# NF4 rounding of feed-forward weights moved from a stage of its own into the attention's steps

## The reference

```python
x1 = layernorm(x  + self_attention(x))      # 16 heads of 32, 8 key heads, rotary, softmax
x2 = layernorm(x1 + cross_attention(x1, ctx))   # keys and values from a 128-wide latent, causal
out = layernorm(x2 + w3 @ (silu(w1 @ x2) * (w2 @ x2)))
```

```python
s = max(abs(block))                       # 11264 blocks in each matrix
q = clip(round((s - mean(s)) * qf), -128, 127)   # qf from the largest of 64 neighbouring s
step = NF4[argmin(abs(block / s - NF4))]   # one of 16 levels
w = step * (q / qf + mean(s))
```

## Time and profile before

| | |
|---|---|
| median of 3 runs | 1345.85 us |
| the profiled execution, its own time | 1342.16 us |
| its span in the trace | 1340.3 us |
| TensorE busy | 1161.6 us (87%) |
| VectorE busy | 802.0 us (60%) |
| ScalarE busy | 414.3 us (31%) |
| GpSimd busy | 233.9 us (17%) |
| first product of the attention stage | 198.59 us |
| first row maximum on VectorE | 228.22 us |

### The profile page before, as it was taken

The page is one execution under the profiler, slowest core; times in us unless marked ns, Lnnn a source line. Parts: engine busy times, 40 slices in busy tenths (PEclk is TensorE's granted clock), DMA queues, the critical chain, the costliest instruction groups (busy, mean ns, idle before and its releaser), DMA issues. The chain is left out here.

```text
span 1340.3 us, 17710 instructions
## 1 busy us (share of the span) xinstructions
PE 1161.6 (87%) x6598; PEld 734.9 (55%) x6613; DVE 802.0 (60%) x1232; ACT 414.3 (31%) x537; POOL 233.9 (17%) x134
## 2 busy tenths in 40 slices
PE   0588777799999999998999999999989399999995
PEld 0144335355454565454565565665655287878784
DVE  7899956456576557567457456466464534545444
ACT  0211111333434423544435434434423131111110
POOL 1522412145226226120001210010001000000000
PEclk9799988699999999999999999999999699999998
DMA  5210012312412313413423524423431510202010
GB/s 187 75 37 24 35 69 65 90 42 54 116 33 71 87 34 108 132 45 88 127 63 107 155 68 115 125 59 97 113 82 49 215 41 0 94 0 94 0 64 31
DMA packets 60778, 103.61 MB, mean 77 GB/s; under 512 B 19622, under 2 KB 20134, under 8 KB 59942
## 3 DMA queue, kind: packets, MB, share of 16 engines
q1 hardware_dynamic: 55286, 85.64, 22.0%
q0 software_dynamic: 4400, 16.78, 3.8%
q10 hardware_dynamic: 1024, 0.26, 0.1%
HBM read 41.29 MB, written 17.04 MB: 44 GB/s over the span
## 5 line engine op out<-in xcount | busy, mean ns | idle before, releaser
L1076 DVE TENSOR_REDUCE att_mx<-att_scores 128x2 f32<-128x1024 f32 (+3 forms) x256 | 262.3, 1025 | 260.3 <-PE att_scores L718 131.4
L959 ACT ACTIVATE att_probs<-att_scores_T 128x1024 f32<-128x1024 f32 (+2 forms) x256 | 214.4, 883 | 252.5 <-PE att_scores_T L741 131.5
L718 PE MATMUL att_scores<-att_k_stack,att_q_stack 96*128 96x512 f32 (+2 forms) x512 | 181.0, 424 | 36.2 <-DVE att_mx L1076 30.8
L759 PE MATMUL att_pv<-att_probs,att_v 128*32 128x512 f32 (+3 forms) x1024 | 207.5, 527 | 0.0
L759 PE MATMUL att_pv<-att_probs,att_ones 128*32 128x512 f32 (+3 forms) x1024 | 207.4, 527 | 0.0
L737 PE MATMUL att_scores_T<-att_q_stack,att_k_stack 97*128 97x512 f32 (+2 forms) x512 | 159.0, 414 | 5.6 <-ACT att_raw L935 5.1
L263 PE MATMUL nf_acc<-nf_steps,nf_ident 128*128 128x512 bf16 x480 | 120.0, 402 | 38.1 <-DVE nf_steps L322 37.3
L718 PEld LDWEIGHTS att_scores<-att_k_stack,att_q_stack 96*128 96x128 f32 x512 | 95.3, 200 | 81.1 <-DVE att_mx L1076 52.5
L641 POOL TENSOR_TENSOR att_o_lo<-att_pv_raw,att_o_hi 128x512 fp32r<-128x512 f32 x32 | 44.5, 1391 | 484.0 <-DVE att_o_hi L1094 484.0
L322 DVE TENSOR_SCALAR nf_steps<-nf_x 128x1536 bf16<-128x1536 bf16 x165 | 122.0, 792 | 10.9 <-PE nf_acc L263 5.1
L737 PEld LDWEIGHTS att_scores_T<-att_q_stack,att_k_stack 97*128 97x128 f32 x512 | 99.4, 198 | 48.6 <-issue 31.1
(11 more groups left out here) (172 smaller groups left out, 1868.1 us busy)
## 6 DMA issues: line engine op xcount, KB each, us to landing
att_q_stack<-att_q_hi SPq DMA_DIRECT2D x256, 64.0 KB, 2.0
att_k_stack<-att_k_hi SPq DMA_DIRECT2D x192, 64.0 KB, 2.0
att_q_stack<-att_q_lo SPq DMA_DIRECT2D x128, 64.0 KB, 2.0
att_k_stack<-att_k_lo SPq DMA_DIRECT2D x96, 64.0 KB, 2.0
nf_nat<-w_nat SPq DMA_DIRECT2D x3, 1408.0 KB, 9.0
w_nf<-nf_w_turned SPq DMA_DIRECT2D x11, 384.0 KB, 2.3
att_y<-x POOLq DMA_DIRECT2D x4, 1024.0 KB, 5.6
x_after_self<-att_y SPq DMA_DIRECT2D x4, 1024.0 KB, 5.8
```

The source lines that it names most:

```text
L718: last = T.matmul(sco[:, r, 0:width], qst[0:96, s, r, P * t:P * t + P], kst[0:96, s, r if crossed(b) else 0, 0:width], start=True, stop=no ...
L759: last = T.matmul(pv[HD * j:HD * j + HD, sums, q0:S], lhs, pt[:, r, at:at + S - q0], start=(t == 0), stop=(t == TT - 1))
L959: A.activation(pt[:, r, 1024 * h:1024 * h + w], bank[:, 0:w], ACT.Exp, scale=SCALE).then_inc(st_free, 1)
L1076: V.tensor_reduce(mx[:, p % 2, :].rearrange("p (r t) -> p r t", r=2)[:, :, t], sco[:, :, 0:P * (t + 1) if crossed(b) else S], AX.X, ALU.ma ...
```

## The change

`nf4_stage` is gone; `build` calls `attention_stage` alone, which now loads and splits the first x and the self attention's weights itself (`x0`, `w0`, two parts of 768 columns each) and takes the largest values of the weight blocks (`largest`, four reduces) between and behind its first three rotations. The scalers are quantised by VectorE inside step (0, 3) and put in order in (0, 7), with two trips through DRAM.

The weights come in a second time from the host, turned (`w_t`). GpSimd multiplies them by reciprocals in 24 pieces of 704 columns at steps 3 to 26 (`divide`), VectorE bounds each piece from below (`bound`), and SyncE stores it to DRAM before it loads the next: one buffer, `xp`. The rounding then runs in 48 rounds, at steps 8 to 27 and 33 to 60. A round loads 32 rows of 1408 columns four times over the partitions (`x4`), so that each group of 32 partitions holds the same weights. One pass compares with four limits, another one in each group; four passes cover 15. `scalar_passes` gives one of four passes to ScalarE (Sign), and three of four at p = 3, 4, 5 of the self blocks; the rest are VectorE's. TensorE adds the steps up in 16 products of 352 columns (`rounding`), VectorE scales (`scale_rounded`), SyncE stores.

```diff
+def round_of(b, p):
+    at = b * NP + p
+    u = at - NP if at < NP + SELF_ROUNDS else at - CROSS_HOME + SELF_ROUNDS if at >= CROSS_HOME else -1
+    return u if 0 <= u < ROUNDS else None
+def scalar_passes(u):
+    b, p = divmod(u + NP, NP)
+    return (0, 1, 3) if u < SELF_ROUNDS and b < B - 1 and p in (3, 4, 5) else (0,)
...
# SyncE
+            def load_piece(i):
+                if i > 0:
+                    sp.wait_ge(piece_out, 16 * i)
+                sp.dma_start(xp, w_t[:, at]).then_inc(piece_in, 16)
+                sp.dma_start(recb, rec_dram[:, None, at].broadcast_to([2, 64, PIECE])).then_inc(piece_in, 16)
+            def load_round(u):
+                if u > 0:
+                    sp.wait_ge(st_full, AT["round", u - 1] + 1)
+                sp.wait_ge(piece_out, 16 * (2 * (u // 4) + 2))
+                sp.dma_start(x4, x_nf[32 * r:32 * r + 32, at][None].broadcast_to([4, 32, CHUNK])).then_inc(rows4_in, 16)
+                if u > 0 and u != SELF_ROUNDS:
+                    store_round(u - 1)
...
# GpSimd, in each step
+                    if p < 2 and b + 1 < B:
+                        lo_of_x(b + 1, p)
+                        nxt = (b + 1, 1) if p == 0 else (b + 2, 0)
+                        pool.wait_ge(x_lo, x_half(b + 1, p))
+                        load_x(*nxt)
...
                     if p in (2, 4, 6):
                         lo_of_o(KT * b + p // 2 - 1)
+                    if piece_of(b, p) is not None:
+                        divide(piece_of(b, p))
# TensorE, behind weigh 0 and 1
+            def rounding(u):
+                pe.wait_ge(over_act, ACT_PASSES[u + 1])
+                pe.wait_ge(over_vec, VEC_PASSES[u + 1])
+                for k in range(4):
+                    for j in range(4):
+                        last = T.matmul(bank[32 * j:32 * j + 32, 0:CW], nsteps[:, 32 * k:32 * k + 32],
+                                        passes[k][:, CW * j:CW * j + CW], start=k == 0, stop=k == 3)
# ScalarE
+                A.activation((over + [x4])[k], x4, ACT.Sign, bias=limits[:, 4 + k:5 + k]).then_inc(over_act, 1)
# VectorE, in each step: passes 1 and 2 behind maxima 1, then
                     if fore:
                         maxima(*fore, 2)
...
+                    if piece_of(b, p) is not None:
+                        bound(piece_of(b, p))
+                    exceeds(u, (3,))
...
+                    early = bool(made(b + 1, p)) or p == 1
+                    if fore and early:
+                        maxima(*fore, 3)
+                    if u is not None:
+                        scale_rounded(u)
+                    if fore and not early:
+                        maxima(*fore, 3)
```

More of the change, by code:

```diff
@@ L828, in project_out, with turn_scalers, make @@
                 last.then_inc(st_full, 1)
-            def make(b, whats, part):
+            def rounding(u):
+                bank = bank_for(("round", u))
+                x4, dqb = home(u)
+                passes = over + [x4]
+                pe.wait_ge(over_act, ACT_PASSES[u + 1])
[4 more added lines that the diff above has]
+                                        passes[k][:, CW * j:CW * j + CW], start=k == 0, stop=k == 3)
+                last.then_inc(st_full, 1)
+            def turn_scalers(unit, t):
+                bank = bank_for(unit)
+                for w in range(NW):
+                    last = T.transpose(bank[0:SB, P * w:P * w + P], t[:, SB * w:SB * w + SB], ident[:, :])
+                last.then_inc(st_full, 1)
+            def make(b, whats, half):
                 if not whats:
                     return
-                what, i = (whats[part], (0, 1)) if len(whats) == 2 else (whats[0], (part,))
+                what, i = (whats[half], (0, 1)) if len(whats) == 2 else (whats[0], (half,))
                 for j in i:
@@ L842, in make @@
                         project(b, what, j)
-            pe.wait_ge(const_ok, 1)
             for what in ("q0", "k0", "q1", "v0"):
-                for part in range(2):
-                    make(0, [what], part)
-            pe.wait_ge(const_ok, CONSTS)
+                for half in range(2):
+                    make(0, [what], half)
+            pe.wait_ge(const_ok, CONSTS - 1)
             for t in range(TT):
@@ L870, in _ @@
                     if crossed(b) and p == 0:
-                        for part in range(2):
-                            make(b, values_of(b), part)
+                        for half in range(2):
+                            make(b, values_of(b), half)
                         maxima(*fore, 2)
@@ new lines, in exceeds, with scale_rounded @@
+            def exceeds(u, ks):
+                for k in ks:
+                    if u is not None and k not in scalar_passes(u):
+                        exceed(u, k)
+            def scale_rounded(u):
+                bank = wait_full(dve, ("round", u))
+                x4, dqb = home(u)
+                base = NF4[0] + sum(STEP[4 * k + h] / 2 for k in scalar_passes(u) for h in range(4))
+                dve.wait_ge(dqb_in, 16 * (u + 1))
+                if u > 0:
+                    dve.wait_ge(w_out, 16 * u)
+                V.scalar_tensor_tensor(wout, bank[:, 0:CW], base, dqb, ALU.add, ALU.mult).then_inc(round_ok, 1)
```

724 lines of the change are left out of this document (402 added, 322 removed).

## The result

| | before | after |
|---|---|---|
| median | 1345.59 us (4 runs) | 1817.2 us (4 runs, 1813.47 to 1821.6) |
| profiled execution, its own time | 1342.16 us | 1813.47 us |
| span in the trace | 1340.3 us | 1811.7 us |

The ratio is 1.35, 95% interval [1.346, 1.354]: slower by 472 us where 53 us of gain were forecast. The time lies far outside the range of 1245 to 1345.

A forecast was written before the change was run, and what follows sets the result against it. It took VectorE to bound the NF4 stage and TensorE to be 90% and 94% busy in self and cross attention. 1342.2 - 166 (start) + 75 (self blocks) + 42 (cross blocks) = 1293 us; range 1245 to 1345.

The forecast's parts named there:

- I take 352 KB to be there 3 us later: Each round's x4 load: there 3 us later, while VectorE wants it 4.4 us after the round.
- rival on a late x4: In the 48 rounds: landing 2.6 us longer loses 1.2 us each, +58, 1351 us, slower; chance 0.08.
- its pass as 1.35 us of work: ScalarE, rounding steps: one pass takes 1.35 us more in a step, and the engine is not full.
- self blocks: Blocks 0 to 3: waits for pieces and rounds add 75 us, bounds 26 and 105.
- cross blocks: 28 rounds there: 28 us plus 14 us for eight steps at p = 2 and 4, +42, bounds 20 and 75.
- The new start: Kernel start without the NF4 stage: first reduce of maxima at 62 us instead of 228, gain 166 us.
- The round: TensorE, each round: 16 products on four column groups take 0.8 us, lower end 0.6, upper end 2.35.
- The rival without overlap: TensorE's column groups don't overlap in bf16: 2.35 us a round instead of 0.8, 74 us more, 1367; chance 0.05.
- GpSimd's product last in its step: Self blocks: `bound`, pass 3, quarter 3's reduce and the round wait behind it; +6.0 us at p = 0.
- By step: Self blocks 1 and 2: added waits step by step, from 1.3 to 6.0 us, together 25 us a block.

The follow-up runs named there:

- e1_rows_first: Changed kernel with x4's copy having 32 rows outermost instead of 4 groups, limit and step tables permuted to match: 1610.4 us, ratio to before 1.198.
- e5_rec_two: e1_rows_first with a piece's reciprocals in two copies of outer dimension 64 instead of one of outer dimension 2: 1474.0 us.
- e3_pass0_last: Changed kernel, x4's copy as it was, with ScalarE's pass 0 moved from in front of exponential 2 to behind exponential 3: 1613.6 us.
- e7_wide_late_pass: e5_rec_two with the scalers once for two rounds in four copies and ScalarE's pass 0 behind exponential 3: 1384.7 us.
- e8_divide_first: e7_wide_late_pass with GpSimd's piece multiplied first (p = 3 to 5: end of the step before) and `bound` before passes 1 and 2: 1323.0 us.
- e9_big_behind: e8_divide_first with the store of y and the load of the cross attention's weights issued behind x4's copy: 1319.8 us.
- e14_best_timed: The kernel of e10_pieces_before unchanged, timed against the kernel before in five rounds: 1299.9 us, ratio 0.969.
- e10_pieces_before: e9_big_behind with SyncE storing a piece and loading the next before it loads the step's stacks: 1294.3 us.
- e11_four_engines: e10_pieces_before with x4's copy alone as in the changed kernel, 4 groups outermost: 1403.0 us.

## Why the prediction was wrong

**The step that failed.** "I take 352 KB to be there 3 us later". It stood in the rival on a late x4, which had 0.08; in the sum the wait for x4 was nothing. The rival named the right place and the price from which it decides, 1.1 us a round. But the 3 us are what the size alone gives by two copies with 128 rows outermost; the prediction shows no other working for them. Measured from issue to first use: 9.6 us in the median of the cross rounds that waited, 15.7 in the self rounds. With the order of two dimensions turned the kernel is 207 us shorter, 4.3 us for each of the 48 rounds (e1_rows_first). The page DMA: Bandwidth & Descriptors of the Trainium skill (Why a DMA increments its semaphore by 16 and not by 1, How many engines) has the rule: the number of engines is the largest up to 16 that divides the slowest dimension, longer than one, of source and destination. For [4, 32, 1408] into 128 partitions that is 4, for the reciprocals' [2, 64, 704] it is 2. Both agree with the traces: a share of 0.14 to 0.28 in the self step above where the wide copy shows 0.80, and the landing of the wide x4 in self blocks at 12.0 us behind the reciprocals as one copy and at 4.1 behind them as two (e5_rec_two). Which engines carried a copy no trace here shows. The diff shows both shapes, so this could have been read before the run.

**What I didn't think of at all.** First, that one slow copy delays the next: the reciprocals were no term of the sum, and x4 behind them took 15.7 us in the median. They cost 136 us (e1_rows_first to e5_rec_two). Second, ScalarE. The prediction counted its pass as 1.35 us of work on an engine that isn't full. It is also a wait in front of exponential 2, on which TensorE's ring of banks hangs; that alone was worth 204 us against the changed kernel (e3_pass0_last) and 89 when x4 was fast.

**The copies are not all of it.** In e5_rec_two both copies are mended and the engines' programs are as forecast, and it takes 1474 us, 181 more than the forecast. Its self blocks are +183 over before where the sum had +75, its cross blocks +109 where it had +42. Of these 181 us the place of pass 0 is 89. Of the 92 that are left (e7_wide_late_pass) 70 are in the self blocks, +145 where the sum had +75, and moving GpSimd's product takes 62 off (e8_divide_first).

**What was right.**
- The new start: 62 forecast, 65.2 measured. The first copy of q0 was 2.9 us later than counted (25.8 for 22.9), the rotations and reduces took what was said: the gain is 163 us, forecast 166.
- The round: 16 products on four column groups in 0.8 us. Here, first at TensorE's lower clock in a self block, then at the higher one:

```profile
246.62 1.07 PE L773 MATMUL att_scores_T<-att_nf_zone,att_nf_steps 128*32 128x352 bf16 x12 [22.46 <-DVE att_nf_home L1208]
247.46 0.53 PE L773 MATMUL att_scores_T<-att_nf_home,att_nf_steps 128*32 128x352 bf16 x4
...
921.63 0.63 PE L773 MATMUL att_scores_T<-att_nf_zone,att_nf_steps 128*32 128x352 bf16 x12
922.08 0.33 PE L773 MATMUL att_scores_T<-att_probs,att_nf_steps 128*32 128x352 bf16 x4
```

  From start to end 1.37 us and 0.78 us. The rival without overlap (2.35) is out.
- GpSimd's product last in its step holds up `bound`, pass 3 and the round: 71 us of waits in the changed kernel, 62 us of time (e8_divide_first).
- That was priced nearly right in some steps and too low where VectorE meets GpSimd's rotation. By step, block 2 of e7_wide_late_pass over block 2 of before, with the forecast in brackets: p = 0 +7.6 (6.0), p = 1 +2.9 (3.3), p = 2 +7.1 (1.3), p = 3 +7.9 (3.3), p = 4 +8.8 (3.5), p = 5 +5.6 (5.2), p = 6 +3.0 (1.3), p = 7 +13.9 (1.3). At p = 2, 3 and 4 `bound` runs into the first product of a rotation: it takes 2.46 us in each of the three, as the row above shows for p = 2. With the piece first (e8_divide_first) p = 2 and p = 4 come down from 21.5 and 23.8 us to 15.2 and 15.9, but p = 3 only from 22.7 to 20.1; why is open. At p = 7 the copies of the cross attention's weights stand in front of x4: with them behind it (e9_big_behind) the step went from 16.5 to 11.4 us, and the next one got longer. In block 1, which has no such copies, p = 7 is still +7.5.

**The sum by itself.** In e14_best_timed the terms are: start -163 (forecast -166), self blocks +10, +28, +24 and +12, together +73 (+75), cross blocks +5, +10, +12 and +17, together +44 (+42), and 2 behind them. From the 1342 of the profiled execution that makes 1298, near the forecast 1293, but it proves the forecast right for no kernel: e14_best_timed has GpSimd's product moved and pass 0 placed late, which the forecast hadn't. With the copies wide and the pass late, but the piece as in the change (e7_wide_late_pass), the self blocks are +145 and the cross blocks +59.

The 523 us between the changed kernel and e10_pieces_before, in the order in which they were taken off: x4's dimension 207, the reciprocals' 136, pass 0 behind the exponentials 89, the piece's place 62, the big copies 3, SyncE's order 25. The order matters: x4's dimension is worth 207 in the first kernel and 103 in the last. Of these kernels only the changed one, e1_rows_first and the last (as e14_best_timed, 1299.9 us in five runs) were timed more than once, so single figures under 10 us are not to be leaned on, and SyncE's order is 20 us by the five runs. How much of the 472 us is the lower clock of TensorE and how much the waits that caused it was not separated.

## What to carry to other kernels

Read the shape of a copy before its size: the same 352 KB were late with 4 groups outermost, in time with 32 rows outermost, and late again behind a copy with 2 outermost. Here turning two dimensions and permuting two small tables gave 207 us. Where a pass that waits for a copy is put in an engine's program, ask what stands behind it on that engine: spare time does not help if the work behind the wait is what TensorE wants. And after a large fault is mended, measure again before pricing the next one, since waits lie on top of each other.

## What the runs showed of the hardware that I had not expected

- A copy of 352 KB landed in 3.6 us in the median with 32 rows outermost (cross blocks of e1_rows_first). With 4 outermost its first use came 7.4 us or more behind its issue in every round that waited for it (9.6 in the median of the cross rounds), and 7.2 or more where the rest was mended (e11_four_engines).
- Copies with few outermost also hold up the queue that issues them. SyncE's issue of the scalers' copy took 0.54 us in cross blocks but 4.27 us in the median and up to 5.66 in self blocks of the changed kernel, where reciprocals and x4 lay before it. With x4 wide it was 2.02 us there (e1_rows_first), with the reciprocals in two copies as well 0.53 (e5_rec_two).
- `bound`, a bf16 pass of VectorE with one operand in SBUF, took 0.34 us in the median and 2.46 us where a product of GpSimd (2.34 us) had begun 0.07 us before it.
